# Router logits with the experts as columns of the result: four plain fp32 products in four column quarters of TensorE

## The chip, the cores and the metric

The kernel runs on one core of one Trainium2 chip. The metric is the device time of one launch in microseconds (us). TensorE is the matrix engine, VectorE, ScalarE and GpSimd work on its results, SyncE issues most of the transfers. In the profile they are PE (with PEld for its weight loads), DVE, ACT, POOL and SP.

## The reference

The input is 32 sequences of 512 tokens with 256 channels. Each sequence goes through two blocks, both as x = x + layernorm(block(layernorm(x))): first a state space block (a projection, a convolution along time, a scan in chunks, an output projection), then a mixture of experts with 16 routed experts and a shared one. The change is in the router:

```
logits = xf @ router_w.T                 # [tokens, 16]
scores = jax.nn.sigmoid(logits)
sb = scores + correction_bias            # 4 groups of 4 experts, best 2 groups, then best 4 experts
...
combine = jnp.zeros((S, E), xf.dtype).at[jnp.arange(S)[:, None], topk_idx].add(w)
g = jnp.einsum('sc,ech->esh', xf, gate_w)
u = jnp.einsum('sc,ech->esh', xf, up_w)
h = jax.nn.silu(g) * u
hw = h * combine.T[:, :, None]
```

## The kernel before, in words

**Stages.** The work of a sequence is cut into parts: p (norm, query projection, rotation), a (state space block, norm, sum), f (router and experts) and g (the end of the expert sum, last norm, store). One pass through `iteration` runs p of sequence i+1, a of sequence i, f of sequence i-1 and g of sequence i-2, all mixed. There are two filling passes and a first one with f, then a loop over 29 passes with all parts, and three emptying ones. A sequence has 12 blocks of 128 hidden units: `gate(j)` and `up(j)` make them, `down(j)` projects them back. `down(10)` and `down(11)` of a pass are done in the next one, as part g.

**Precision.** A matrix product is made of three one-pass products (type fp32r) of rounded high parts and low parts: high by high, high by low, low by high (`split_mm`). So each operand is rounded by ScalarE (its high part) and subtracted by VectorE (its low part). A few products are plain fp32: the states (`state`, `from_state`), `diagonal`, `CB` and the sums of `cumulate` (lines 1393 to 1395). Transpositions are products with an identity.

**The router.** `ffn_by_channel(0)` and `(1)` transpose the normed activations of each half of the tokens, ScalarE's `f_high` and VectorE's `f_low` make fTh and fTl of them. `logits(0)` and `logits(1)` use `narrow`: for each tile of 128 tokens and each half of the channels the tokens are the weights of the array, and the router's 32 columns (high and low parts of 16 experts) or 16 columns (high parts only) stream through. These are 16 products per sequence (lines 1374 and 1376). VectorE's `route_logits` adds the two column groups in two small instructions, ScalarE takes the tanh, VectorE picks the experts.

**What sets the order.** Every engine runs its own list, written out in `iteration` of that engine, and waits on counted semaphores. On TensorE these are waits for an operand (`read_out`, `wait_ge`) and for a PSUM bank to be free (`slot`): part p has one bank, a three, f two, in the order of P_SLOTS, A_SLOTS and F_SLOTS. The tuples FREED list in which order ScalarE and VectorE free the banks.

**The seam between two passes.** TensorE ends a pass with `gate(11)`, `h_by_channel(1)` and `up(11)`. The transposed h of the next sequence becomes hTh (ScalarE, `h_high`) and hTl (VectorE, `h_low`); `project_z(0, 0)` of the next pass waits until both halves of hTl are made. VectorE's `up(11)` multiplies the last hidden block out of PSUM.

```
if c == 0 and n == 0:
    pe.wait_ge(s_hT, 2)
    pe.sem_inc(s_hT, -2)
```

On VectorE the end of the list is `norm_q(1); h_low(0)`, `add_x(1)`, `h_low(1)`, `up(11)`; on ScalarE `gate(10)`, `h_high(0); h_high(1)`, `gate(11)`, `norm_x1(0)`, `round_hidden(10)`, `norm_x1(1)`, `round_hidden(11)`. TensorE begins a pass with `project_z(0, 0)`, `project_z(1, 0)`, `ffn_by_channel(0)`, which reads what `norm_x1(0)` made, `project_x(4)` and `ffn_by_channel(1)`.

Of the kernel before, what the change touches and what calls it, by code (L numbers as in the profile page):

```python
# [12 lines left out]
P = 128  # L13
# [19 lines left out]
def build(nc, x, wq_t, wzx_t, conv_w, conv_b, dt_bias, a_log, d_param, npw, ngw, wo_t,  # L33
# [6 lines left out]
    with ctx:  # L40
# [85 lines left out]
        junk = (xc[:, 4, :], xdec[:, 1, :])  # L126

# [10 lines left out]
        def rows(ap, dims, offset=0):  # L138
# [14 lines left out]
            ("za0", "DVE", "ACT"), ("za1", "DVE", "ACT"), ("xc4", "ACT", "ACT"), ("za2", "DVE", "ACT"),  # L153
            ("xc5", "ACT", "ACT"), ("za3", "DVE", "ACT"), ("xc0", "ACT", "ACT"), ("xc1", "ACT", "ACT"),
            ("xc2", "ACT", "ACT"), ("zb0", "ACT", "ACT"), ("acs", "DVE", "DVE"), ("zb1", "ACT", "ACT"),
            ("xc3", "ACT", "ACT"), ("Bt", "ACT", "ACT"), ("zb2", "ACT", "ACT"), ("CB", "ACT", "ACT"),
            ("xt0", "DVE", "DVE"), ("xt1", "DVE", "DVE"), ("st0", "DVE", "DVE"), ("zb3", "ACT", "ACT"),
            ("yd0", "DVE", "DVE"), ("yo1", "DVE", "DVE"), ("st1", "DVE", "DVE"), ("xt2", "DVE", "DVE"),
            ("yd1", "DVE", "DVE"), ("yo2", "DVE", "DVE"), ("yT0", "ACT", "DVE"), ("st2", "DVE", "DVE"),
            ("yd2", "DVE", "DVE"), ("xt3", "DVE", "DVE"), ("out0", "", "DVE"), ("yT1", "ACT", "DVE"),  # L160
            ("yo3", "DVE", "DVE"), ("yT2", "ACT", "DVE"), ("yd3", "DVE", "DVE"), ("out1", "", "DVE"),
            ("yT3", "ACT", "DVE")]
        F_SLOTS = [
            ("fT0", "ACT", "DVE"), ("fT1", "ACT", "DVE"), ("logits", "", "DVE"), ("G0", "ACT", "ACT"),
            ("U0", "DVE", "DVE"), ("G1", "ACT", "ACT"), ("U1", "DVE", "DVE"), ("G2", "ACT", "ACT"),
            ("U2", "DVE", "DVE"), ("G3", "ACT", "ACT"), ("G4", "ACT", "ACT"), ("U3", "DVE", "DVE"),
            ("cT", "ACT", "ACT"), ("U4", "DVE", "DVE"), ("G5", "ACT", "ACT"), ("U5", "DVE", "DVE"),
            ("G6", "ACT", "ACT"), ("U6", "DVE", "DVE"), ("G7", "ACT", "ACT"), ("U7", "DVE", "DVE"),
            ("G8", "ACT", "ACT"), ("U8", "DVE", "DVE"), ("G9", "ACT", "ACT"), ("U9", "DVE", "DVE"),
# [190 lines left out]
        def _(sp):  # L360
# [73 lines left out]
            def iteration(i, p, a, f, g):  # L434
                if f: save_x1(i - 1)
                if a: decay_store(); decay_rows(0); decay_rows(1)
                if f: combine_store(); combine_rows(0)
                if p: load_next(i + 1)
                if f: combine_rows(1)
                if a: decay_rows(2); decay_rows(3)  # L440
# [1224 lines left out]
```

## Time and profile before

| | us |
|---|---|
| median of 3 runs | 3214.55 |
| lowest and highest | 3213.54, 3217.93 |
| the profiled execution | 3218.34 |
| its span, first to last instruction | 3216.4 |
| TensorE busy | 3116.9 (97%) |
| VectorE busy | 2393.1 (74%) |
| GpSimd busy | 2033.7 (63%) |
| ScalarE busy | 1931.1 (60%) |

The busy time of an engine is the time in which it has at least one instruction under way. Matmuls overlap, so the time that one takes of the engine is the distance between its start and the start of the next one, not its duration.

### The profile page before, as it was taken

Reading aid. Unit: us, or ns where it says so; the run is one execution under the profiler, and the core shown is the slowest. Engines: PE = TensorE matmul, PEld = TensorE weight load, DVE = VectorE, ACT = ScalarE, POOL = GpSimd, SP = SyncE. Lnnn points to the kernel's source line nnn. Section 1 sums busy time; section 2 is a strip of 40 time slices with the busy share of each in tenths; the row PEclk is TensorE's granted clock in tenths of the full one; section 3 lists DMA queues with packets and bytes.
Section 4 is the critical chain, followed back from the end, with each engine's and each line's share of the span. In section 5 each row is a group of like instructions: output and inputs, shape, how many; then the busy total and the mean of one; then the engine's idle time right before and its main releaser. Section 6 shows DMA issues by size and latency. Waiting matters only on the chain.

```text
span 3216.4 us, 62379 instructions
## 1 busy us (share of the span) xinstructions
PE 3116.9 (97%) x19648; PEld 2723.4 (85%) x19648; DVE 2393.1 (74%) x5104; ACT 1931.1 (60%) x4146; POOL 2033.7 (63%) x2311
## 2 busy tenths in 40 slices
PE   3699999999999999999999999999999999999997
PEld 3588888888888888888888888888888888888886
DVE  3777777777777777777777777777777777777772
ACT  3566665566665566665666665666665656665652
POOL 0466666766666776666776666776666776666764
PEclk9799999999999999999999999999999999999999
DMA  3122222222222222222222222222222222222221
GB/s 109 40 70 80 66 59 74 73 76 79 66 60 75 72 77 78 66 60 74 72 78 76 66 63 72 72 79 76 66 65 71 71 79 76 66 67 69 71 80 40
DMA packets 143434, 227.33 MB, mean 71 GB/s; under 512 B 18977, under 2 KB 88353, under 8 KB 143393
## 3 DMA queue, kind: packets, MB, share of 16 engines
q1 hardware_dynamic: 126496, 210.06, 19.9%
q0 software_dynamic: 16896, 16.78, 4.0%
q8 instruction: 20, 0.33, 0.0%
q14 instruction: 22, 0.17, 0.0%
HBM read 174.87 MB, written 35.13 MB: 65 GB/s over the span
## 4 chain that ended last, share of the span: by engine, by line
PE 94%; POOL 1%; DMA 0%; DVE 0%; ACT 0%; issue 0%; SPq 0%; POOLq 0%; ACTq 0%; DVEq 0%
PE fpb L1325 33%; PE apb L1325 19%; PE acc L1504 17%; PE apb L1450 7%; PE apb L1334 4%; PE ppb L1325 3%; PE apb L1435 3%; PE apb L1442 2%; PE ppb L1344 2%; PE apb L1422 1%; PE fpb L1374 1%; PE fpb L1344 1%; PE fpb L1376 1%; PE fpb L1483 0%; PE apb L1395 0%; POOL hid L541 0%
## 5 line engine op out<-in xcount | busy, mean ns | idle before, releaser
L546 POOL TENSOR_TENSOR hidL<-hid,hidH 128x512 fp32r<-128x512 f32 x384 | 545.8, 1421 | 216.8 <-ACT hidH L801 207.5
L1015 DVE SCALAR_TENSOR_TENSOR xc<-apb,cw,xc 128x511 f32<-128x511 f32 (+2 forms) x576 | 427.8, 748 | 67.8 <-ACT xc L714 39.5
L1504 PE MATMUL acc<-WDH,hidH 128*128 128x256 f32 x1536 | 458.2, 298 | 6.2 <-POOLq L548 5.9
L801 ACT CAST hidH<-hid 128x512 fp32r<-128x512 f32 x384 | 236.1, 615 | 353.6 <-POOL hid L541 288.7
L1504 PE MATMUL acc<-WDH,hidL 128*128 128x256 f32 x1536 | 432.0, 281 | 0.0
L1504 PE MATMUL acc<-WDL,hidH 128*128 128x256 f32 x1536 | 431.5, 281 | 0.0
L541 POOL TENSOR_TENSOR hid<-hid,cb 128x512 f32<-128x512 f32 x256 | 347.2, 1356 | 81.8 <-DVEq L1136 43.7
L1134 DVE TENSOR_TENSOR hid<-hid,fpb 128x512 f32<-128x512 f32 x384 | 261.1, 680 | 135.4 <-PE fpb L1325 125.2
L1325 PE MATMUL fpb<-fTh,UH 128*128 128x512 f32 x768 | 336.1, 438 | 0.8 <-ACTq L793 0.8
L732 ACT ACTIVATE seg<-seg,acs 128x128 f32<-128x128 f32 x1024 | 313.8, 389 | 10.2 <-ACT cb L782 5.9
L1325 PE MATMUL fpb<-fTh,GH 128*128 128x512 f32 x768 | 317.5, 413 | 0.0
L1504 PEld LDWEIGHTS acc<-WDH,hidH 128*128 128x128 f32 x1536 | 290.6, 189 | 22.9 <-POOLq L548 8.6
L1325 PE MATMUL fpb<-fTh,GL 128*128 128x512 f32 x768 | 303.9, 396 | 0.0
L1325 PE MATMUL fpb<-fTh,UL 128*128 128x512 f32 x768 | 303.7, 395 | 0.0
L1325 PE MATMUL fpb<-fTl,UH 128*128 128x512 f32 x768 | 302.3, 394 | 0.0
L1325 PE MATMUL fpb<-fTl,GH 128*128 128x512 f32 x768 | 302.3, 394 | 0.0
L1504 PEld LDWEIGHTS acc<-WDL,hidH 128*128 128x128 f32 x1536 | 291.1, 189 | 12.8 <-issue 7.4
L790 ACT ACTIVATE hid<-fpb 128x512 f32<-128x512 f32 x384 | 228.5, 595 | 122.1 <-PE fpb L1325 84.1
L1504 PEld LDWEIGHTS acc<-WDH,hidL 128*128 128x128 f32 x1536 | 290.5, 189 | 0.0
L1450 PEld LDWEIGHTS apb<-xdt,seg 128*128 128x128 f32 x2048 | 245.9, 193 | 10.6 <-issue 5.1
L1450 PE MATMUL apb<-xdt,seg 128*128 128x64 f32 x2048 | 245.0, 273 | 3.6 <-DVE seg L1052 3.6
L1052 DVE TENSOR_TENSOR seg<-seg,CBs 128x1024 f32<-128x1024 f32 x128 | 195.5, 1528 | 41.9 <-ACT seg L732 32.5
(194 smaller groups left out, 8672.1 us busy)
## 6 DMA issues: line engine op xcount, KB each, us to landing
seg<-acs_row SPq DMA_DIRECT2D x128, 512.0 KB, 4.2
cb<-c_row SPq DMA_DIRECT2D x512, 128.0 KB, 2.9
xsP<-in_x SPq DMA_DIRECT2D x32, 512.0 KB, 3.6
xc<-qrot SPq DMA_DIRECT2D x32, 512.0 KB, 3.4
xc<-in_x SPq DMA_DIRECT2D x32, 512.0 KB, 4.3
out<-xc SPq DMA_DIRECT2D x32, 512.0 KB, 3.0
out<-xn POOLq DMA_DIRECT2D x32, 512.0 KB, 6.0
ZL_loaded<-in_wzx_t SPq DMA_DIRECT2D x2, 512.0 KB, 5.7
```

Of the source, the lines that this page charges most:

```text
L541: G.tensor_tensor(hid[:, j % 2, :], hid[:, j % 2, :], cb[:, r % 2, :], ALU.mult).then_inc(sem["routed_ready"], 1)
L546: own.do(G.tensor_tensor(hidL[:, j % 2, :], hid[:, j % 2, :], hidH[:, j % 2, :].bitcast(fp32), ALU.subtract))
L732: ins = A.activation(seg[:, c % 2, h, :], seg[:, c % 2, h, :], ACT.Exp, bias=acs[:, 0, c * HS + h:c * HS + h + 1])
L790: own.do(A.activation(hid[:, j % 2, :], bank(f"G{j}")[:], ACT.Silu))
L801: A.copy(hidH[:, j % 2, :], hid[:, j % 2, :]).then_inc(sem["hidden_high"], 1)
L1015: ins = V.scalar_tensor_tensor(xc[:, b, s:], src[:, 0:T - s], cw[:, b, TAPS - 1 - s:TAPS - s], xc[:, b, s:], ALU.mult, ALU.add)
L1052: V.tensor_tensor(seg[:, c % 2, :, :], seg[:, c % 2, :, :], CBs[:, c, :].unsqueeze(1).broadcast_to([P, HS, P]), ALU.mult).then_inc(sem["m_ ...
L1134: own.do(V.tensor_tensor(hid[:, j % 2, :], hid[:, j % 2, :], bank(f"U{j}")[:], ALU.mult))
L1325: ins = nc.tensor.matmul(dst, l, r, start=n == 0, stop=n == total - 1)
L1334: ins = nc.tensor.transpose(b[:, t * P:(t + 1) * P], src(t), ident[:])
L1450: ins = nc.tensor.matmul(b[:, hs], seg[:, c % 2, h, :], xdt[:, c % 2, hs], start=True, stop=True)
L1504: ins = nc.tensor.matmul(dst, l[:, w, tk], r[:, j, :], start=j == 0 and t % 2 == 0 and n == 0, stop=j == HB - 1 and n == 2, skip_group_che ...
```

## The change

The two calls of `logits` per sequence become one. The router's weights are now the stationary operand (32 columns: 16 high parts and 16 low parts), and all 512 tokens stream through. There are four such products, plain fp32: fTh and fTl, each with two halves of the channels. Product n writes rows 32n to 32n+31 of one PSUM bank, so each has its own quarter of the array's columns, and none is added to another in PSUM. ScalarE copies the bank [128, 512] to SBUF (`evac_logits`, into a free half of xdec), TensorE transposes it by four tiles of 128 tokens (`logits_by_token`, bank LT), and one VectorE sum over the eight parts of each expert (4 products by high and low) gives the logits. `narrow` goes.

With it the order lists of all engines are other ones, and so are the bank lists. The core of the diff, with the ends and beginnings of the lists:

```diff
-            def logits(s):
-                b = bank("logits") if s else slot("logits")
-                read_out(f"fT{s}")
-                ins = narrow(b, fTh, fTl, R, E, (2 * s, 2 * s + 1))
-                if s:
-                    ins.then_inc(sem["logits_made"], 1)
+            def logits():
+                b = slot("logits")
+                for s in range(2):
+                    read_out(f"fT{s}")
+                for n, (part, k) in enumerate(((fTh, 0), (fTh, 1), (fTl, 0), (fTl, 1))):
+                    ins = nc.tensor.matmul(b[n * 2 * E:(n + 1) * 2 * E, :], R[:, k, :].bitcast(fp32), part[:, k, :].bitcast(fp32),
+                                           start=True, stop=True)
+                fill("logits", ins)
+
+            def logits_by_token():
+                b = slot("LT")
+                read_out("logits")
+                fill("LT", transposes(b, lambda t: lgT[:, t * P:(t + 1) * P]))
...
+            def evac_logits():
+                filled(act, "ACT", "logits")
+                free("f", "logits", A.copy(lgT, bank("logits")[:]))
...
             def route_logits():
-                dve.wait_ge(sem["logits_made"], 1)
-                parts = bank("logits")[:, 0:2 * NT * E].rearrange("p (t a e) -> p t a e", t=NT, a=2)
-                own.do(V.tensor_copy(msk[:].rearrange(te, t=NT), parts[:, :, 0, :]))
-                own.do(V.tensor_tensor(msk[:].rearrange(te, t=NT), msk[:].rearrange(te, t=NT), parts[:, :, 1, :], ALU.add))
-                free("f", "logits")
+                filled(dve, "DVE", "LT")
+                parts = bank("LT")[:].rearrange("p (t n e) -> p t e n", t=NT, e=E)
+                own.do(V.reduce_sum(msk[:].rearrange(te, t=NT), parts, AX.X))
+                free("f", "LT")
                 dve.sem_inc(sem["logits_ready"], 1)
```

TensorE's list, its beginning:

```diff
+                if f: ffn_by_channel(0)
                 if w: weights_split(KD + 1)
-                if a: project_z(0, 0); project_z(1, 0)
-                if f: ffn_by_channel(0)
-                if a: project_x(4)
+                if a: project_z(0, 0)
                 if f: ffn_by_channel(1)
-                if g: down(10)
-                if f: settled("ffn_in_ready")
-                if a: project_z(2, 0); project_x(5)
-                if g: down(11); settled("last_split")
-                if f: logits(0); logits(1)
-                if a: project_z(3, 0); project_x(0)
-                if f: gate(0)
...
+                if a: project_z(1, 0)
+                if f: settled("ffn_in_ready")
+                if a: project_x(4); project_x(5)
+                if f: logits(); gate(0); logits_by_token()
+                if a: project_x(0)
+                if g: down(10)
+                if f: gate(1)
+                if a: project_z(0, 1); project_z(2, 0)
+                if f: up(0)
+                if a: project_z(1, 1); project_z(3, 0)
+                if g: down(11); settled("last_split")
```

Its end stays: `gate(11)`, `h_by_channel(1)`, `up(11)`. VectorE's end, and ScalarE's:

```diff
                 if p: norm_q(1); h_low(0)
                 if a: add_x(1)
                 if w: split_low(11)
+                if f: up(11)
                 if p: h_low(1)
-                if f: up(11)
...
                 if f: gate(10)
-                if p: h_high(0); h_high(1)
+                if p: h_high(0)
                 if f: gate(11)
+                if p: h_high(1)
                 if a: norm_x1(0)
```

In the middle ScalarE's list also changes: the four `exp_seg` of a pass stood in two groups between table loads (0 and 1, 2 and 3) and stand in three (0; 1 and 2; 3), so that a pass has eight table loads instead of six. On SyncE the load of `decay_rows(1)` stands ahead of `decay_rows(0)`, and the loads of the combine rows stand later among the others.

## Rows read from the trace of the kernel before

**Rows 1.** The page: busy time of TensorE, and the chain that ended last.
```profile
PE 3116.9 (97%) x19648; PEld 2723.4 (85%) x19648; DVE 2393.1 (74%) x5104; ACT 1931.1 (60%) x4146; POOL 2033.7 (63%) x2311
...
PE 94%; POOL 1%; DMA 0%; DVE 0%; ACT 0%; issue 0%; SPq 0%; POOLq 0%; ACTq 0%; DVEq 0%
```

**Rows 2.** Busy time in one pass: stretch, length, engines, granted clock, DMA share, GB/s.
```profile
1016.05:1112.45 96.40, 96.36 (x614) 84.50 (x615) 74.19 (x159) 59.80 (x130) 63.35 (x73) 1.00 0.24 71
```

**Rows 3.** TensorE's groups by line: the products of the logits.
```profile
L1376 PE MATMUL fpb<-R,fTl 128*128 128x16 f32 x256 | 58.2, 256 | 0.0
L1374 PE MATMUL fpb<-R,fTh 128*128 128x32 f32 x256 | 55.8, 252 | 0.4 <-DVE fTl L1118 0.4
```

**Rows 4.** TensorE in order of time around the logits: start, duration, engine, line, operation.
```profile
1024.88 0.18 PE L1374 MATMUL fpb<-R,fTh 128*128 128x32 f32 x1
...
1026.59 0.37 PE L1325 MATMUL apb<-ZH,hTh 128*128 128x264 f32 x1
1026.79 0.28 PE L1325 MATMUL apb<-ZL,hTh 128*128 128x264 f32 x1
1026.91 0.29 PE L1325 MATMUL apb<-ZH,hTl 128*128 128x264 f32 x1
```

**Rows 5.** TensorE in order of time: plain fp32 products of 512 columns.
```profile
1063.02 1.02 PE L1435 MATMUL apb<-S,xc 128*128 128x512 f32 x2
1063.87 1.02 PE L1442 MATMUL apb<-xdec,Btok 128*128 128x512 f32 x2
```

**Rows 6.** TensorE in order of time: around a product with 32 active columns.
```profile
1038.02 0.39 PE L1394 MATMUL apb<-ad,ones 128*128 128x32 f32 x2
1038.34 0.41 PE L1395 MATMUL apb<-upper,ad 128*32 128x128 f32 x2
1038.67 0.50 PE L1325 MATMUL fpb<-fTh,GH 128*128 128x512 f32 x1
1039.01 0.39 PE L1325 MATMUL fpb<-fTl,GH 128*128 128x512 f32 x1
```

**Rows 7.** TensorE in order of time: the seam of two passes.
```profile
1015.39 0.39 PE L1325 MATMUL fpb<-fTl,UH 128*128 128x512 f32 x1
1015.61 0.40 PE L1325 MATMUL fpb<-fTh,UL 128*128 128x512 f32 x1
1016.05 0.36 PE L1325 MATMUL apb<-ZH,hTh 128*128 128x264 f32 x1
...
1017.60 0.60 PE L1344 MATMUL fpb<-ident,xdt 128*128 128x128 f32 x4
1017.95 0.48 PE L1325 MATMUL apb<-hTh,ZH 128*128 128x512 f32 x1
1018.27 0.39 PE L1325 MATMUL apb<-hTl,ZH 128*128 128x512 f32 x1
```

**Rows 8.** VectorE in order of time: the seam; in brackets idle time and its releaser.
```profile
1011.02 0.69 DVE L1134 TENSOR_TENSOR hid<-hid,fpb 128x512 f32<-128x512 f32 x1 [0.81 <-PE fpb L1325]
1011.95 0.62 DVE L981 TENSOR_SCALAR xn<-qrot,rq 128x256 f32<-128x256 f32 x2 [0.24 <-DVE hid L1134]
...
1015.26 0.69 DVE L992 TENSOR_TENSOR hTl<-ppb,hTh 128x512 fp32r<-128x512 f32 x1
1016.12 0.69 DVE L1134 TENSOR_TENSOR hid<-hid,fpb 128x512 f32<-128x512 f32 x1 [0.17 <-PE fpb L1325]
```

**Rows 9.** ScalarE in order of time: the seam.
```profile
1014.64 0.59 ACT L703 CAST hTh<-ppb 128x512 fp32r<-128x512 f32 x1 [2.67 <-PE ppb L1344]
1015.13 0.60 ACT L790 ACTIVATE hid<-fpb 128x512 f32<-128x512 f32 x1
1015.92 1.09 ACT L768 ACTIVATE xdt<-xc,nb,rstd 128x256 f32<-128x256 f32 x2 [0.19 <-ACT hid L790]
```

**Rows 10.** ScalarE's groups by line: table loads, the rounding of yT, the copy of cT.
```profile
L655 ACT ACT_TABLE_LOAD x97 | 124.5, 1283 | 8.0 <-ACT hid L790 5.3 <-POOL one L466 1.4
...
L754 ACT CAST yTh<-apb 128x512 fp32r<-128x512 f32 x128 | 74.6, 583 | 90.8 <-PE apb L1334 88.9
...
L782 ACT COPY cb<-fpb 16x512 f32<-16x512 f32 x32 | 18.4, 575 | 47.5 <-PE fpb L1483 47.5
```

More of the change, by code:

```diff
@@ L152, in build @@
         A_SLOTS = [
[L153 to L157, printed above, removed]
@@ L166, in build @@
[L166 to L169, printed above, removed]
-            ("G10", "ACT", "ACT"), ("U10", "DVE", "DVE"), ("G11", "ACT", "ACT"), ("U11", "DVE", "DVE")]
+            ("fT0", "ACT", "DVE"), ("fT1", "ACT", "DVE"), ("logits", "ACT", "ACT"), ("G0", "ACT", "ACT"),
@@ L1546, in iteration @@
[L1546 to L1547 removed]
+                if a: settled("ad_ready"); project_x(3)
+                if f: up(2); gate(3); down(0); settled("acc_free"); gate(4)
+                if a: project_z(3, 1)
+                if f: down(1)
                 if a: CB(); x_by_token(0)
[L1549 removed]
+                if f: up(3); down(2)
+                if a: B_by_token()
+                if f: gate(5)
                 if a: x_by_token(1)
[L1551 removed]
@@ L1552, in iteration @@
-                if a: state(0); project_z(3, 1); diagonal(0)
-                if f: up(5)
-                if a: from_state(1); state(1)
-                if f: down(3)
-                if a: x_by_token(2)
-                if f: gate(6)
+                if f: combine_by_expert()
+                if a: state(0); diagonal(0)
+                if f: down(3); settled("c_ready")
+                if a: from_state(1)
+                if f: up(4)
+                if a: x_by_token(2); state(1); y_by_channel(0)
@@ L1558, in iteration @@
+                if f: up(5); gate(6)
+                if p: x_by_channel(0)
                 if a: diagonal(1); from_state(2)
-                if f: up(6); down(4)
-                if a: y_by_channel(0)
+                if f: down(4)
+                if a: state(2); x_by_token(3)
+                if f: up(6)
+                if a: settled("a_out_ACT", "xdec_ready")
                 if f: gate(7)
-                if a: state(2)
-                if f: up(7)
-                if a: settled("xdec_ready"); diagonal(2); x_by_token(3)
@@ L1573, in iteration @@
+                if a: project_out(1)
+                if f: gate(9)
                 if p: project_q(0)
-                if a: project_out(1)
-                if f: down(6); up(8)
-                if a: y_by_channel(2); diagonal(3)
+                if a: diagonal(3); y_by_channel(2)
+                if f: up(8)
+                if a: settled("m_ready")
                 if f: down(7)
-                if a: settled("m_ready")
                 if p: x_by_channel(1)
-                if f: gate(9)
+                if a: project_out(2)
```

250 lines of the change are left out of this document (122 added, 128 removed).

## The prediction

> **What bounds the kernel now.** I read the busy times first: TensorE has work under way for 97% of the span, and 94% of the chain that ended last runs through it [rows 1]. A share of busy time says little with overlapping matmuls, so I next took one pass of the loop by windows. It lasts 96.40 us, TensorE is busy for 96.36 of it at a granted clock of 1.00 (its upper level, 2.4 GHz), VectorE for 74.19, ScalarE 59.80, GpSimd 63.35 [rows 2]. The reader is to see that TensorE's list is the clock of the kernel: what it gains or loses in a pass comes 30 times, and what other engines gain or lose counts only where it makes TensorE wait. Then I looked in order of time for starts that are further apart than the same kind of product needs. There is one such place per pass worth naming, the seam: the last record of `up(11)` starts at 1015.61, products of 512 columns follow each other at 0.23, so the next could start at 1015.84; `project_z(0, 0)` starts at 1016.05 [rows 7], 0.10 after the end of the second hTl at 1015.95 [rows 8]. So 0.21 us per pass are lost there, to exactly the operand that the new lists touch.
>
> **Removed: sixteen narrow products.** They start at 1024.88 and the second product of the next projection starts at 1026.79; without them it would start one pitch of 0.12 after 1024.88, at 1025.00 [rows 4]. That is 1.79 us per sequence (0.112 each, far below their duration of 0.25 [rows 3]).
>
> **Added: four transpositions.** Four like them and the product behind them take 1017.60 to 1018.27, 0.67 us, of which 0.23 are that product's [rows 7]: 0.44 us.
>
> **Added: four plain fp32 products.** Such a product is two records of the trace. With 512 columns two records take 1063.02 to 1063.87, 0.85 us, so 0.43 each [rows 5]. How four in different quarters stand to each other no row shows. The ends: one behind the other, 8 x 0.43 = 3.44 us; all four at once, 2 x 0.43 = 0.86 us. I take a value between. The nearest row is the sum with 32 active columns: its two records use the same quarter and do not run together [rows 6], as they can't, since they need the same cells. If TensorE also starts its products strictly in the order of the list, as every row shows it to, the second record of product 0 waits for the first, the first of product 1 starts beside it and not before, and so on: a staircase of five steps, 5 x 0.43 = 2.15 us.
>
> The Trainium skill (TensorE: Matmul & The Clock Gate, Part 3: Packing small matmuls) says that matmuls in different column quarters run together at a few ns from each other, and that starts and ends keep program order; no row here has two quarters in use. Taken for the product as a whole that is the end of 0.86; taken for each record it is the staircase.
>
> **Added: into and out of 32 columns.** From 1038.02 to 1039.01, 0.99 us, lie two records at 0.112 (the pitch of the narrow ones), two of 128 columns at a quarter of 0.43, 0.107, and one of 0.23 [rows 6]: 0.67 by sum. The other 0.32 us is what the change of shape costs around them: the array empties before and after, and the next weights aren't loaded ahead. That comes once per sequence.
>
> **Sum of the router on TensorE.** 2.15 + 0.32 + 0.44 - 1.79 = +1.12 us per sequence, times 32 = +36 us. With the ends: 0.86 gives -0.17, or -5 us; 3.44 gives +2.41, or +77 us.
>
> **Moved: the seam.** This is the part that I am surest of. `up(11)` stays the last work of TensorE's pass, and VectorE now multiplies it before it makes the second half of hTl. The last record of U11 starts at 1015.61; VectorE takes it up at 1016.12 and ends at 1016.81 [rows 7, 8]. What follows such a multiplication starts 0.24 after its end (1011.71 to 1011.95 [rows 8]), so hTl is made from 1017.05 to 1017.74 by its 0.69, and `project_z(0, 0)` starts 0.10 later, at 1017.84 instead of 1016.05. Of the work that follows, only `ffn_by_channel(0)`, 0.44 us, is now ahead of it. Loss per seam: 1.79 - 0.44 = 1.35 us. Its cover would be other TensorE work, but the list has none that doesn't need hTl. `ffn_by_channel(0)` itself must start by 1017.40 to stay in that shadow. It needs `norm_x1(0)`, which ended at 1017.01 [rows 9]; now `gate(11)` goes first on ScalarE, from about 1014.3, then `h_high(1)`, so the norm ends near 1016.6. Not late. There are 30 seams whose earlier pass has both parts: +40 us. Ends: if ScalarE's gate is not early and the whole row of rounding, gate and norm is late, fT0 ends later by 0.3 and it is 1.65 (+50); if VectorE took the second operation with no gap, 1.1 (+33).
>
> **Other engines.** ScalarE gets a copy of 128x512 (0.58 for a like one) and two more table loads at 1.28 [rows 10]: 3.1 us per pass, 63 of 96 us busy. It must be done within `gate(0)`'s 1.4 us after the products: about 0.2 to see the bank and 0.6 for itself; and where the queue still holds `conv_first(5)` (0.78) it ends before the staircase does. VectorE's two instructions of 0.22 become one over 512 elements, 0.2 to 0.5 more, with 22 us free per pass. `down(11)` ends some 10 us later in a pass, and with it the last moments, the last norm and the release of the accumulators; `down(0)` waits for that, stands later too, and I count its release a good microsecond ahead. SyncE's `decay_rows(0)` lands one transfer later, ahead of an `exp_seg(0)` that stands behind a table load. I walked the list from the seam to `diagonal(0)` with the durations of the rows, and find each operand ready by 0.2 us or more; the tightest is `diagonal(0)` itself. I take 0 for all this; the ends are -0.15 us per pass (the idle of 0.36 that sums of pitches leave in 96.40, without the seam's 0.21) and +0.6 (one operation of ScalarE or VectorE late, once), -5 to +18 us. Filling and emptying the pipeline may move some us either way.
>
> **The sum.** 3218.34 + 36 + 40 = 3294 on the profiled execution, which is 3.8 above the median; on the median 3291 us, +2.4%.
>
> **The rivals.**
> A. The four quarters run one behind the other: +77 instead of +36, 3332 us. For it: no row shows two products at once, and every plain fp32 record takes its full 0.43. Against: different cells, different PSUM rows.
> B. All four run at once, products as wholes: -5 instead of +36, 3250 us. For it: there is no shared cell; against: it needs the first record of product 1 to start before the second of product 0.
> C. Faster: the seam is covered. This is one mechanism: hTl lands within 0.65 us of the last start of U11 (0.23 plus `ffn_by_channel(0)`), since what `h_low(1)` waits for was done long before; then the 0.21 of today goes as well, 30 x 0.21 = 6, and with all quarters at once 5 more: 3203 us. It decides at 1016.28 on the clock of rows 7. For it: the transposition was moved into that gap. Against: VectorE works in order, and U11 is seen by it only at 1016.12.
> D. No change: B, and the seam is no wider than today's 0.21, 3214.55 - 5 = 3210 to 3220 us. It needs C's mechanism by half.
> E. A second wait of more than 0.6 us in each pass on top: 3340 and above.
>
> **How the numbers follow.** Forecast (staircase and seam) 0.40, own range 3275 to 3312; A 0.22; B 0.23; C 0.06; D 0.04; E 0.05. The range 3242 to 3340 holds the forecast, A and B and leaves out C, D and E, 0.15. What a measurement of this kernel can tell from no change is about 0.2%, 6.4 us. Faster 0.07, same 0.05, slower 0.88.
>
> **What will show it.** Right: in the profile after, TensorE's first `project_z` of a pass starts 0.1 behind the second hTl of VectorE, that hTl stands behind the multiplication of U11, and the page shows a wait of TensorE of more than a microsecond per pass at that place (for hTl, or for `ffn_by_channel(0)`'s input). A pass is 98.9 us. The eight records of the logits start in five steps of 0.43, with two starts close together at the inner ones; eight steps are A, two groups of four are B. The transpositions take 0.44 and the first product behind the router comes 0.1 late with its load. Wrong: a pass under 97 us; hTl of `h_low(1)` ahead of U11's product; new waits at `diagonal`, `down(0)` or `logits_by_token` that are larger than the seam.

## The result, and the profile after

The changed kernel took 3300.0 us (median of 4 runs, 3299.9 to 3301.5); the kernel before took 3216.2 us (4 runs, 3213.5 to 3220.3). The ratio is 1.026, with a 95% interval of 1.0243 to 1.0278. It is slower, and 9 us from the forecast of 3291. The profiled execution has a span of 3298.1 us at a mean granted clock of 0.99, where the one before had 3216.4: 81.7 us more.

The busy times on the page after. TensorE's share has fallen from 97% to 95%, though it is busy for 26 us more; the rest of the loss is idle time.

```profile
span 3298.1 us, 62218 instructions
...
PE 3142.8 (95%) x19520; PEld 2679.0 (81%) x19520; DVE 2466.6 (75%) x5072; ACT 2059.7 (62%) x4242; POOL 2045.4 (62%) x2311
```

One pass of the loop, in the columns of [rows 2]:

```profile
1038.07:1136.80 98.73, 97.13 (x610) 83.08 (x610) 76.70 (x159) 63.87 (x133) 63.88 (x73) 1.00 0.24 70
```

A pass is 98.73 us instead of 96.40, at the same granted clock of 1.00, so 2.33 us longer; 30 of them are 70 us. From the last logits to the end of the program it takes 88.4 us where it took 76.3: 12 us. These two are the whole difference. Of the 2.33 us of a pass, 1.56 are idle TensorE: it is busy for 97.13 of 98.73.

TensorE in order of time at the seam, to be read against [rows 7]:

```profile
1134.67 0.40 PE L1335 MATMUL fpb<-fTh,UL 128*128 128x512 f32 x1
1135.98 0.66 PE L1354 MATMUL fpb<-ident,xdt 128*128 128x128 f32 x4 [0.91 <-DVEq L936]
1136.90 0.36 PE L1335 MATMUL apb<-ZH,hTh 128*128 128x264 f32 x1 [0.26 <-issue]
```

`project_z(0, 0)` starts 2.23 us after the last record of U11, where before it started 0.44 after. The forecast was 1015.61 to 1017.84, also 2.23. The bracket shows something the forecast didn't have: `ffn_by_channel(0)` (the four transpositions) waits too, 0.91 us idle, until VectorE has given a PSUM bank back.

VectorE and then ScalarE in the same stretch, against [rows 8] and [rows 9]:

```profile
1135.18 0.69 DVE L1139 TENSOR_TENSOR hid<-hid,fpb 128x512 f32<-128x512 f32 x1 [0.99 <-PE fpb L1335]
1136.11 0.69 DVE L998 TENSOR_TENSOR hTl<-ppb,hTh 128x512 fp32r<-128x512 f32 x1 [0.24 <-DVE hid L1139]
...
1138.77 0.17 DVE L1003 TENSOR_TENSOR dr<-apb,dtb 128x8 f32<-128x8 f32 x1 [1.97 <-DVEq L317]
```

```profile
1137.47 0.62 ACT L802 CAST hidH<-hid 128x512 fp32r<-128x512 f32 x1 [0.28 <-POOL hid L542]
1139.16 0.59 ACT L771 CAST fTh<-fpb 128x512 fp32r<-128x512 f32 x1 [1.08 <-ACTq L317]
1139.65 0.39 ACT L739 ACTIVATE zs<-apb 128x256 f32<-128x256 f32 x1
```

VectorE does what the new list says: U11's product first, from 1135.18, then, 0.24 after its end, hTl until 1136.80; the projection starts 0.10 later. ScalarE's last operation of the pass is the rounding of U11's hidden values at 1137.47, for it comes behind the product on VectorE and the weighting on GpSimd. Then ScalarE stands for 1.08 us while the semaphores of the pass are settled, and only at 1139.16 does it begin the first work of the next pass, the rounding of fT0.

The router on TensorE, against [rows 4]:

```profile
1141.44 0.40 PE L1335 MATMUL apb<-hTh,ZL 128*128 128x512 f32 x1
1141.77 0.62 PE L1479 MATMUL fpb<-fTh,R 128*32 128x512 f32 x2
1141.78 0.62 PE L1479 MATMUL fpb<-fTl,R 128*32 128x512 f32 x2
1142.22 0.60 PE L1479 MATMUL fpb<-fTh,R 128*32 128x512 f32 x2
1142.24 0.60 PE L1479 MATMUL fpb<-fTl,R 128*32 128x512 f32 x2
1142.77 0.50 PE L1335 MATMUL fpb<-fTh,GH 128*128 128x512 f32 x1
1143.11 0.39 PE L1335 MATMUL fpb<-fTl,GH 128*128 128x512 f32 x1
```

Each row with "x2" joins two records. Taken singly they start at 1141.769, .776, .783, .789 and then at 1142.223, .229, .236, .243: two groups of four, 7 ns apart inside a group. The first record of every product runs, all four at once, and then the second of every product. From the last start before them (1141.44) to the second product behind them (1143.11) it takes 1.67 us; with no router it would be two pitches of 0.23, so the products and the change of shape cost 1.20 us. With 0.44 for the transpositions and without the 1.79 of the narrow products that is -0.15 us per sequence. There was no staircase.

What TensorE waits for in the other places (engine, line, releaser; total us, times, longest):

```profile
PE fpb L1354 <- DVEq L936: 28.3, 31, 0.9
PE ppb L1335 <- DVE xTl L967: 13.0, 33, 2.3
```

In order of time, `from_state(2)` and the first product of `project_q(1)`:

```profile
1092.70 1.10 PE L1435 MATMUL apb<-S,xc 128*128 128x512 f32 x2
...
1122.67 0.36 PE L1335 MATMUL ppb<-WQH,xTh 128*128 128x256 f32 x1 [0.26 <-DVE xTl L967]
```

The table of waits puts 0.26 of idle time at `project_q(1)`, but idle time begins where the modelled end of a matmul lies. Measured by starts, as at the seam, the product starts 0.50 us later than it does where nothing holds it (0.03 behind the last transposition, in e7_xlow_first below). `from_state(2)`, at 1092.70, shows no bracket at all and comes 0.43 us behind the last record of `diagonal(1)` where it comes 0.11 behind it in the kernel before; with 0.02 more at its second record it is 0.34 late. Both stand behind VectorE. VectorE in order of time, and GpSimd in the same stretches:

```profile
1072.22 3.33 DVE L1188 TENSOR_TENSOR gt<-gt,eq 128x64 f32<-128x64 f32 x1
...
1088.16 2.12 DVE L1058 TENSOR_TENSOR seg<-seg,CBs 128x1024 f32<-128x1024 f32 x1
1090.20 1.58 DVE L1069 TENSOR_TENSOR S<-S,el 128x512 f32<-128x512 f32 x1
1091.81 0.69 DVE L1072 TENSOR_TENSOR S<-S,apb 128x512 f32<-128x512 f32 x1
...
1118.40 2.48 DVE L1110 SCALAR_TENSOR_TENSOR xc<-xc,rstd 128x256 f32<-128x256 f32 x2 [0.31 <-DVE hid L1139]
```

```profile
1072.80 2.66 POOL L502 TENSOR_SCALAR_AFFINE_SELECT seg<-seg 128x1024 f32<-128x1024 f32 x2
...
1087.90 1.30 POOL L542 TENSOR_TENSOR hid<-hid,cb 128x512 f32<-128x512 f32 x1
1089.15 2.08 POOL L502 TENSOR_SCALAR_AFFINE_SELECT seg<-seg 128x1024 f32<-128x1024 f32 x1
...
1117.89 1.28 POOL L518 TENSOR_TENSOR zs<-zs,xD 128x512 f32<-128x512 f32 x1
1119.13 1.47 POOL L542 TENSOR_TENSOR hid<-hid,cb 128x512 f32<-128x512 f32 x1
```

Three of these groups of VectorE take far longer than their kind does elsewhere in the same trace (the product of seg and CBs 1.22, that of S and el 0.69, the two of xc and rstd 0.87), and each lies beside instructions of GpSimd. The operands of `from_state(2)` and `project_q(1)` come out of these lists. But the stretch is not new. The kernel before has it in the same places, `new_state(1)` and `add_x(0)`:

```profile
1065.06 1.45 DVE L1052 TENSOR_TENSOR seg<-seg,CBs 128x1024 f32<-128x1024 f32 x1
1066.43 1.77 DVE L1063 TENSOR_TENSOR S<-S,el 128x512 f32<-128x512 f32 x1
...
1096.22 0.69 DVE L961 TENSOR_TENSOR xTl<-ppb,xTh 128x512 fp32r<-128x512 f32 x1 [0.79 <-ACT xTh L691]
1096.83 2.27 DVE L1104 SCALAR_TENSOR_TENSOR xc<-xc,rstd 128x256 f32<-128x256 f32 x2
```

What is new is what stands in front. Before, xTl was made ahead of the slow `add_x(0)`, now it is made behind it. And `times_dt(2)`, two instructions of 0.69 us, stood behind `new_state(1)` and now stands ahead of `decay_CB(1)`, whose product of seg and CBs takes 2.12 where it took 1.45.

### The profile page after: what moved, and what is told of

It reads as the page before. It is cut to its first block and busy times, and to the rows that moved or that the text cites. A ratio compares the mean times of both kernels' runs of the same rounds, so it can differ in the third digit from the quotient of the medians.

```text
span 3298.1 us, 62218 instructions
## 1 busy us (share of the span) xinstructions
PE 3142.8 (95%) x19520; PEld 2679.0 (81%) x19520; DVE 2466.6 (75%) x5072; ACT 2059.7 (62%) x4242; POOL 2045.4 (62%) x2311
## 5 line engine op out<-in xcount | busy, mean ns | idle before, releaser
L547 POOL TENSOR_TENSOR hidL<-hid,hidH 128x512 fp32r<-128x512 f32 x384 | 526.0, 1370 | 306.9 <-ACT hidH L802 280.0
L1513 PE MATMUL acc<-WDH,hidH 128*128 128x256 f32 x1536 | 453.9, 296 | 11.3 <-POOLq L549 10.8
L802 ACT CAST hidH<-hid 128x512 fp32r<-128x512 f32 x384 | 237.5, 618 | 240.0 <-POOL hid L542 163.3
L1139 DVE TENSOR_TENSOR hid<-hid,fpb 128x512 f32<-128x512 f32 x384 | 262.3, 683 | 163.7 <-PE fpb L1335 153.8
L542 POOL TENSOR_TENSOR hid<-hid,cb 128x512 f32<-128x512 f32 x256 | 336.8, 1316 | 46.3 <-DVEq L1141 32.5
```

The costliest lines, as they stand in the source:

```text
L542: G.tensor_tensor(hid[:, j % 2, :], hid[:, j % 2, :], cb[:, r % 2, :], ALU.mult).then_inc(sem["routed_ready"], 1)
L547: own.do(G.tensor_tensor(hidL[:, j % 2, :], hid[:, j % 2, :], hidH[:, j % 2, :].bitcast(fp32), ALU.subtract))
L802: A.copy(hidH[:, j % 2, :], hid[:, j % 2, :]).then_inc(sem["hidden_high"], 1)
L1139: own.do(V.tensor_tensor(hid[:, j % 2, :], hid[:, j % 2, :], bank(f"U{j}")[:], ALU.mult))
L1513: ins = nc.tensor.matmul(dst, l[:, w, tk], r[:, j, :], start=j == 0 and t % 2 == 0 and n == 0, stop=j == HB - 1 and n == 2, skip_group_che ...
```

## The experiments

Each kernel was timed on one chip with the kernel before: e1 to e4 together, e5 to e8 together, e9 to e11 together. The kernel before took 3219.1, 3219.2 and 3220.0 us there. "Pass" is the mean distance of the logits' first records over the 29 full passes, "tail" the time from the last logits to the end. In this measure the kernel before has 96.40 and 76.3 us, the changed one 98.73 and 88.4. "By starts" means that the distance of two starts on TensorE is compared with the distance of the same two where nothing holds them.

### e1_seam_vector: the swap undone on VectorE

```
-                if f: up(11)
                 if p: h_low(1)
+                if f: up(11)
```

> The changed kernel with one swap on VectorE: h_low(1) again ahead of up(11). Everything else as changed. Theory 1 (two waits lie on top of each other at the seam: project_z(0, 0) waits for hTl, and ffn_by_channel(0) ahead of it waits until VectorE has read U11, because the added bank LT moved U11 and fT0 to the same PSUM bank): the second stays, fT0 starts 1.3 us after the last start of U11 as now, and only the 0.47 us between fT0 and project_z goes, 30 x 0.47 = 14 us: 3286 us against 3300. Rival (only hTl holds the seam, as the prediction had it): 30 x 1.35 = 40 us less, 3260 us.

Measured: 3302.6 us, ratio 1.0261 (1.0246 to 1.0277), pass 98.78. Neither theory came: nothing came back. `ffn_by_channel(0)` starts 1.45 us after the last U11 (1430.35 to 1431.80), 0.14 later than in the changed kernel, since VectorE now frees U11's bank second. `project_z(0, 0)` follows it closely, 0.36 us earlier after U11 than in the changed kernel. But `project_x(5)`, further down TensorE's list, gives 0.41 back. It starts 5.57 us after the last U11 (at 1435.92); in the changed kernel it starts 5.61 after it (1134.67 to 1140.28), without a wait of its own. Something else holds it at the same place, and the next experiment shows what.

### e2_seam_both: the swap undone on VectorE and TensorE

```
-                if f: ffn_by_channel(0)
...
-                if a: project_z(0, 0)
-                if f: ffn_by_channel(1)
-                if a: project_z(1, 0)
+                if a: project_z(0, 0); project_z(1, 0)
+                if f: ffn_by_channel(0); ffn_by_channel(1)
```

> The swap on VectorE of the last kernel and on TensorE project_z(0, 0) and project_z(1, 0) ahead of ffn_by_channel(0) and (1), which is the seam of the kernel before. Theory 1 (hTl and the bank of U11 are all that the seam costs): a pass is 1.35 us shorter than 98.72, 97.37, and the kernel takes 3300 - 40 = 3260 us. Rival (the projections ahead delay fT0, its rounding and so the logits): part comes back as a wait at the logits, 3275 us or more.

Measured: 3301.4 us, ratio 1.0261 (1.0247 to 1.0275), pass 98.79. Again nothing came back, as the rival's "3275 us or more" had it, though the seam itself closed and the wait is not at the logits. TensorE in order of time:

```profile
1431.02 0.40 PE L1335 MATMUL fpb<-fTh,UL 128*128 128x512 f32 x1
1431.87 0.36 PE L1335 MATMUL apb<-ZH,hTh 128*128 128x264 f32 x1 [0.45 <-issue]
...
1436.59 0.49 PE L1335 MATMUL apb<-hTh,ZH 128*128 128x512 f32 x1 [0.75 <-ACT zs L739]
```

`project_z(0, 0)` now starts 0.85 after the last U11 instead of 2.23, and 4.7 us later `project_x(5)` waits 0.9 for the bank that ScalarE's `silu_z(0, 0)` frees (it starts at 1436.15, after the rounding of U11's values at 1433.97 and that of fT0 at 1435.66). That instruction hangs on the chain U11, VectorE's product (L1139), GpSimd's weighting (L542), ScalarE's rounding (L802), and the 1.08 us of settling. From the last U11 to ScalarE's first work of the next pass this chain takes 4.64 us here and in e1_seam_vector, 4.49 in the changed kernel and 4.50 in the kernel before. `project_x(5)` starts 5.57 us after U11 again. So the seam has two holders, hTl and this chain, and they end within 0.04 us of each other (5.61 and 5.57): taking the first away leaves the wait to the second.

### e3_router_alone: only the new router, in the kernel before

```
-                if f: logits(0); logits(1)
+                if f: logits()
...
-                if f: gate(0)
+                if f: logits_by_token(); gate(0)
```

It also has the copy on ScalarE, the sum on VectorE and the additional bank; all lists keep the order of the kernel before, but that `route_logits` stands behind the last moments.

> The kernel before with the new router alone: its own order lists, with the four products at the place of the old ones, the copy behind silu_z(2, 0), the transpositions after project_x(0), the sum after the last moments. Theory 1 (the router itself is cheaper on TensorE, 1.10 + 0.44 instead of 1.79 us, and all of the loss is order): a pass of 96.15 us instead of 96.40, the kernel 8 us faster than before, 3207 us. Rival (the longer way of the logits over ScalarE and TensorE costs waits wherever it stands): a pass of 96.4 or more, no gain.

Measured: 3214.2 us (11 runs), ratio 0.9985 (0.9976 to 0.9994), pass 96.26, tail 77.3. The records of the router stand as in the changed kernel, in two groups of four that start at 1312.99 and 1313.44.

The router by itself is a gain of 0.14 us per pass (0.25 was expected), 5 us in all, as rival B of the prediction had it. The whole loss of the changed kernel therefore comes from the new order of the lists.

### e4_other_waits: the waits of `project_q(1)` and `from_state(2)`, on e2_seam_both

```
-                if a: times_dt(2); decay_CB(1)
+                if a: decay_CB(1)
...
-                if a: new_state(1)
+                if a: new_state(1); times_dt(2)
...
+                if p: x_low(1)
                 if a: add_x(0)
...
-                if p: x_low(1)
```

The list in which VectorE frees the banks is changed to match.

> The last-but-one kernel (the changed one with the seam of before) and two more edits on VectorE: x_low(1) ahead of add_x(0), and times_dt(2) behind new_state(1) instead of ahead of decay_CB(1). Theory 1 (what is left of the loss per pass is two waits of TensorE, 0.50 us at project_q(1) for xTl and 0.39 us at from_state(2) for the state, both behind VectorE instructions that ran 0.9 to 1.6 us longer while GpSimd was busy): a pass of 96.5 us, 27 us less than with the seam alone, 3233 us. Rival (the waits move to the next product, since VectorE's list is as full as before): less than 10 us.

Measured: 3296.6 us, ratio 1.0244 (1.0230 to 1.0258), pass 98.53. The rival came. Both waits went, 0.50 and 0.35, and a new one came, for `times_dt(2)` now frees its bank late:

```profile
PE apb L1450 <- DVE xD L1053: 11.0, 31, 1.7
```

By starts it is 0.57 us at `diagonal(1)`. So 0.85 less 0.57 should have given 0.28; the pass gave 0.26. In this kernel the product of S and el at `new_state(1)` takes 0.68 us and that of seg and CBs 1.23, so the place of `times_dt(2)` and the stretch went together, and this run doesn't tell them apart.

### e5_seam_three_lists: ScalarE's list as well, on e2_seam_both

```
-                if f: f_high(0)
                 if a: silu_z(0, 0)
-                if f: f_high(1)
+                if f: f_high(0); f_high(1)
...
-                if p: h_high(0)
+                if p: h_high(0); h_high(1)
...
-                if p: h_high(1)
```

> The changed kernel with the seam of before on VectorE (h_low(1) first) and TensorE (both projections first), as in the second experiment, and now on ScalarE too: h_high(1) ahead of gate(11), and at the start of a pass silu_z(0, 0) ahead of f_high(0). Theory 2 (the second experiment won nothing since project_x(5), now fourth in TensorE's pass, needs the bank that silu_z(0, 0) frees, and that stands behind the chain U11, VectorE's up(11), GpSimd's combine(11), ScalarE's round_hidden(11), 1.1 us of semaphore work at the end of ScalarE's pass and f_high(0); only the f_high, 0.5 us, is taken out of it here): a pass of 98.3 us, 3287 us. Rival (hTl at project_z and the order of f_high were the two missing pieces): a pass of 97.4, 3260 us.

Measured: 3291.3 us, ratio 1.0224 (1.0208 to 1.0240), pass 98.47. `project_z(0, 0)` has its 0.45 after the last U11 again and the wait of `project_x(5)` is gone, but two others hold the head of the pass, the second `ffn_by_channel` and the logits, 0.64 and 0.31 us by starts:

```profile
1429.14 0.63 PE L1352 MATMUL fpb<-ident,xdt 128*128 128x128 f32 x4 [0.44 <-ACT xdt L765]
...
1432.92 0.62 PE L1477 MATMUL fpb<-fTh,R 128*32 128x512 f32 x2 [0.23 <-DVE fTl L1122]
```

That is close to the 98.3 of theory 2. Three lists have the seam of before and still a pass is only a third of a microsecond shorter: what is missing is work of TensorE to lie beside the chain (the next kernel shows it).

### e6_down_ahead: `down(10)` back to the head of the pass, on e5_seam_three_lists

```
-                if f: ffn_by_channel(0); ffn_by_channel(1)
+                if f: ffn_by_channel(0)
+                if a: project_x(4)
+                if f: ffn_by_channel(1)
+                if g: down(10)
...
-                if a: project_x(4); project_x(5)
+                if a: project_x(5)
...
-                if g: down(10)
```

> The last kernel, and TensorE has down(10) between ffn_by_channel(1) and project_x(5), with project_x(4) ahead of ffn_by_channel(1), as the kernel before has it: 1.4 us of work while ScalarE gets to silu_z(0, 0). Theory 2: project_x(5) doesn't wait any more, a pass is 1.35 us shorter than the changed one, 97.4 us, 3260 us. Rival (some other chain through the emptying of the lists holds 98.7 us, and TensorE's waits only move): 3285 us or more.

Measured: 3257.3 us, ratio 1.0122 (1.0107 to 1.0138), pass 97.37, tail 86.2. The 12 records of `down(10)` are 1.4 us of work that needs nothing from this chain, and with them ahead of `project_x(5)` the waits of the head are gone. From e2_seam_both to here a pass loses 1.42 us: this is the size of the seam that the forecast had (1.35), got back by four edits together. Each of the first three was worth nothing or 0.32; whether `down(10)` at the head would do with fewer of them beside it was not tested.

### e7_xlow_first: `x_low(1)` ahead of `add_x(0)`, on e6_down_ahead

```
+                if p: x_low(1)
                 if a: add_x(0)
...
-                if p: x_low(1)
```

> The last kernel with x_low(1) ahead of add_x(0) on VectorE. Theory: the wait of 0.50 us at project_q(1) is the whole cost of add_x(0) standing ahead, which GpSimd stretches from 0.9 to 2.5 us; it goes: 15 us less than the last kernel, 3245 us. Rival (add_x(0) later moves the wait to its own readers, or the pass is held by another chain): less than 5 us.

Measured: 3241.1 us, ratio 1.0071 (1.0057 to 1.0085), pass 96.86, tail 84.2. The pass loses 0.51, what `project_q(1)` waited; its first product comes 0.50 us earlier behind the transpositions, and no other distance of two starts changes by more than 0.02. VectorE in order of time in this kernel:

```profile
1391.50 0.69 DVE L965 TENSOR_TENSOR xTl<-ppb,xTh 128x512 fp32r<-128x512 f32 x1 [1.72 <-ACT xTh L688]
1392.11 0.88 DVE L1108 SCALAR_TENSOR_TENSOR xc<-xc,rstd 128x256 f32<-128x256 f32 x2
```

Both gains are there: xTl comes first, and the two instructions of `add_x(0)`, 2.48 us in the changed kernel, now take 0.88: the instructions of GpSimd beside them work on two elements per partition, not on 512. One edit changed both the place and the stretch. In the place of the changed kernel, the 2.27 us of the kernel before would still have made `project_q(1)` some 0.3 late (an estimate: 0.50 less 0.21), and 0.88 not at all. The wait took both: the old stretch and the new place.

### e8_mask_later: GpSimd's `mask(2)` behind `rest(4)`, on e7_xlow_first

```
-                if a: mask(2)
                 if f: rest(4)
-                if a: decayed(2)
+                if a: mask(2); decayed(2)
```

> The last kernel with GpSimd's mask(2) behind rest(4) instead of ahead of it. Theory (VectorE's instructions with two operands in SBUF stand still while GpSimd works in SBUF; mask(2) met decay_CB(1), 2.1 instead of 1.2 us, and the scaling of the state, 1.6 instead of 0.7, and that is the wait of 0.39 us at from_state(2)): decay_CB(1) takes 1.2 us again, from_state(2) waits less than 0.1, 9 to 12 us less than the last kernel. Rival (rest(4) comes into the same place and stretches the same instructions): no change.

Measured: 3249.3 us, ratio 1.0098 (1.0083 to 1.0114), pass 97.18. It is 8 us slower than e7_xlow_first, where the theory had a gain and the rival no change. VectorE in the stretch of `new_state(1)`:

```profile
1362.08 2.10 DVE L1055 TENSOR_TENSOR seg<-seg,CBs 128x1024 f32<-128x1024 f32 x1
1364.11 1.75 DVE L1066 TENSOR_TENSOR S<-S,el 128x512 f32<-128x512 f32 x1
```

Another instruction of GpSimd takes the place of the mask (the one of `rest(4)`, from 1363.90 for 1.42 us), and the product of S and el takes 1.75 us instead of 1.57 (0.69 alone). The product of seg and CBs keeps its 2.1 us, so it was not the mask that stretched it. GpSimd works for two thirds of the pass; to push one instruction away brings the next. The wait of `from_state(2)` grew from 0.34 to 0.52, which is 0.18 of the 0.33 that the pass lost. Two more were stretched further on in the pass, a product of seg and CBs from 1.38 to 2.25 and the second one of S and el from 0.69 to 1.49, and a `gate` behind them starts 0.10 late.

### e9_one_quarter: all four products in one quarter, on e3_router_alone

```
+                    m = n % 1
-                    ins = nc.tensor.matmul(b[n * 2 * E:(n + 1) * 2 * E, :], R[:, k, :].bitcast(fp32), part[:, k, :].bitcast(fp32),
-                                           start=True, stop=True)
+                    ins = nc.tensor.matmul(b[m * 2 * E:(m + 1) * 2 * E, :], R[:, k, :].bitcast(fp32), part[:, k, :].bitcast(fp32),
+                                           start=n < 1, stop=n >= 3, skip_group_check=True)
```

The four products are summed in PSUM, and VectorE's sum has two terms in place of eight.

> The kernel before with the new router alone (third experiment, a pass of 96.25 us), but all four plain fp32 products go to rows 0 to 31, one quarter of the array's columns, and are added in PSUM; the sum on VectorE takes two parts instead of eight. Theory (products in one quarter follow each other, and the gain of the four quarters is that they run at once): eight records at 0.43, 3.44 us instead of 0.87; a pass of 98.8 us, the kernel 82 us slower than the third experiment, 3296 us. Rival (the time is that of streaming 512 tokens with 32 columns, whatever the quarters): no difference.

Measured: 3296.1 us, ratio 1.0239 (1.0224 to 1.0255), pass 98.78, as the theory had it. Eight records follow one another, at 0.453 us once and then at 0.429:

```profile
1343.60 1.90 PE L1476 MATMUL fpb<-fTh,R 128*32 128x512 f32 x4
1345.34 1.88 PE L1476 MATMUL fpb<-fTl,R 128*32 128x512 f32 x4
```

### e10_two_quarters: two products in each of two quarters, on e3_router_alone

```
+                    m = n % 2
-                    ins = nc.tensor.matmul(b[n * 2 * E:(n + 1) * 2 * E, :], ...
+                    ins = nc.tensor.matmul(b[m * 2 * E:(m + 1) * 2 * E, :], ...
-                                           start=True, stop=True)
+                                           start=n < 2, stop=n >= 2, skip_group_check=True)
```

Two products are added in PSUM in each quarter, and VectorE's sum has four terms.

> The same with two quarters: products 0 and 2 in the first, 1 and 3 in the second, added in PSUM. The order of the list alternates quarters. Theory A (records of different quarters run at once, and a record waits only for those of its own quarter): 4 steps of 0.43, 1.72 us; a pass of 97.1 us, 28 us slower than the third experiment. Theory B (TensorE keeps the order of the list record by record, which with four quarters it did not): a longer staircase, 5 steps or more, 2.15 us and more, 42 us or more slower.

Measured: 3240.8 us, ratio 1.0068 (1.0053 to 1.0084), pass 97.10, theory A. The records come in four steps of 0.43, two at each step, 7 ns apart:

```profile
1322.86 1.05 PE L1476 MATMUL fpb<-fTh,R 128*32 128x512 f32 x4
1323.74 1.03 PE L1476 MATMUL fpb<-fTl,R 128*32 128x512 f32 x4
```

With one, two and four quarters in use a pass is 98.78, 97.10 and 96.26 us. Between them the eight records take eight, four and two steps: 4 x 0.43 = 1.72 and 2 x 0.43 = 0.86 less, and 1.68 and 0.84 are measured. Quarters of the array divide the time, record by record.

### e11_one_pass: the same with the rounded type, in one quarter, on e9_one_quarter

```
-                    ins = nc.tensor.matmul(b[m * 2 * E:(m + 1) * 2 * E, :], R[:, k, :].bitcast(fp32), part[:, k, :].bitcast(fp32),
+                    ins = nc.tensor.matmul(b[m * 2 * E:(m + 1) * 2 * E, :], R[:, k, :], part[:, k, :],
```

The parts are kept in the rounded type already, so here they are multiplied without being read as plain fp32.

> The same as e9 with one quarter, but the products are of the one-pass type fp32r, as everywhere else in the kernel (all operands are rounded parts already, so nothing is lost but low by low rounding). Four records of 512 columns at 0.233 each: 0.93 us instead of the 0.87 of the four quarters. Theory: the same pass as the third experiment within 0.1 us, 96.25 to 96.35, so 0 to 3 us slower. Rival (with 32 columns a one-pass product costs as much as a plain record, or its weights are loaded in the open each time, 0.03 to 0.1 us): 96.4 to 96.6.

Measured: 3206.4 us, ratio 0.9961 (0.9947 to 0.9975), pass 96.00. It is the fastest kernel of all, 8 us ahead of e3_router_alone, where the theory had it up to 3 us behind: the theory kept the cost of the change of shape, and there is none here.

```profile
1308.09 0.29 PE L1510 MATMUL acc<-WDH,hidL 128*128 128x256 f32 x1
1308.21 0.63 PE L1476 MATMUL fpb<-fTh,R 128*32 128x512 f32 x2
1308.68 0.63 PE L1476 MATMUL fpb<-fTl,R 128*32 128x512 f32 x2
1309.15 0.29 PE L1331 MATMUL apb<-ZH,hTh 128*128 128x264 f32 x1
1309.27 0.29 PE L1331 MATMUL apb<-ZL,hTh 128*128 128x264 f32 x1
```

Each product is one record of 0.233 us, four take 0.93, and nothing is lost ahead of or behind them: 0.12 from the record before, 0.12 to the second one after. The four plain fp32 products are faster by themselves, 0.87 for all, but pay some 0.32 for the change of shape around them.

## Why the prediction was right, and where it wasn't

The time came within 9 us, in the predicted direction and range. That is in part luck. The sum behind it did not hold in the same way: the seam was right to a few hundredths of a microsecond; the router came out 41 us lower than forecast, and the two terms that were put at nothing or left open came to 46 us. The two errors cancel: with the router as measured and the other two at nothing, the time would have been rival B's 3250 us.

| term | forecast, us | measured, us | by |
|---|---|---|---|
| router, 32 sequences | +36 | -5 | e3_router_alone, e9 to e11 |
| seam, 30 passes | +40 | +40 (1.35 each by starts; 1.42 given back) | trace after; e6_down_ahead |
| other waits, 30 passes | 0 (-5 to +18) | +34 (1.13 each) | 0.50 and 0.34 by starts, 0.29 by subtraction; 0.51 given back by e7_xlow_first |
| emptying the pipeline | "some us either way" | +12 | trace after |
| sum | +76 | +81 (span: +81.7) | |

The 0.29 is what is left of the 2.33 us of a pass when the rest is taken off, so the sum of the last column agrees with the span by construction; it is no check of the terms.

**The bound.** Right. TensorE's list was the clock, and each of the eleven kernels has a span that differs from the one before by its pass times 30 and its tail, to within 4 us.

**The router.** Every term but one was right: 0.44 for the transpositions, 0.32 for the shape (e3_router_alone: 1.19 in all less 0.87), 1.79 for what was removed. The step that failed is "if TensorE also starts its products strictly in the order of the list ... a staircase of five steps". The start of product 1 doesn't wait for the second record of product 0: all first records run together and then all second ones, 0.87 in place of 2.15. This was rival B. The argument against it ("it needs the first record of product 1 to start before the second of product 0") was no row but a reading of how records must stand; the trace shows exactly that exchange.

The Trainium skill (TensorE: Matmul & The Clock Gate, Part 3: Packing small matmuls) says that matmuls in different column quarters run together a few ns apart. The trace agrees, with 7 ns. Its other statement, that starts keep program order, holds for products here, but not for their records.

**The seam.** Right in place and size, and the cause that was named is there: VectorE takes U11 first, hTl stands 0.24 behind, `project_z(0, 0)` starts 2.23 us after the last U11, as forecast. Two things were missed. With one bank more in the list of the FFN, U11 and the first transposition fall on the same bank, so `ffn_by_channel(0)` isn't the free cover it was taken for; it starts 1.08 us late by starts (0.91 of it idle), but still inside the shadow of the same wait, and the sum didn't change. And the seam was treated as one wait with one cause. The experiments show two holders, VectorE's order and the chain through GpSimd and ScalarE into the next pass: the first alone gives nothing back (e1, e2), four edits together 1.42 (e6). In the changed kernel the two end within 0.04 us of each other at `project_x(5)`. The named cause explains the 1.35, but the chain that was not seen would have cost as much by itself, with `down(10)` gone from the head of the pass. That the size came out right says little for the claim that hTl alone sets it.

**Other engines at nothing.** This step failed. The walk through the list found every operand ready with 0.2 us or more to spare; three came late instead. The prediction shows no duration of `add_x(0)`, `decay_CB(1)` or `new_state(1)`, so which ones the walk took can't be told. The trace of the kernel before had them: 2.27 us for the two instructions of `add_x(0)`, where the other two of the same line take 0.87, and 1.77 for the product of S and el. In the new order `add_x(0)` stands ahead of xTl and takes 2.48 us, and xTl comes late for `project_q(1)`: 0.50 per pass, shown by e7_xlow_first. Ahead of `from_state(2)` the products of seg and CBs and of S and el take 2.12 and 1.58 us, 0.48 more together than before, and the 1.3 us of `times_dt(2)` are new there: 0.34 per pass. Which of the two is its cause stays open: e4_other_waits moves `times_dt(2)` and removes wait and stretch together, but makes another wait; e8_mask_later lengthens both the product and the wait. The remaining 0.29 (some 0.1 of it at `diagonal(0)`) was not tested.

**The tail.** The forecast left it open. It became 12 us. In the emptying passes `down` waits for GpSimd's `rest`, 3.09 us in one place and 1.67 in another:

```profile
3240.90 0.58 PE L1513 MATMUL acc<-WDH,hidH 128*128 128x256 f32 x1 [3.09 <-POOLq L549]
```

All such waits of a run come to 10.8 us, where they come to 5.9 in the kernel before, so they account for 5 of the 12. That the tail belongs to the order and not to the router is shown by e3_router_alone, whose tail is 77.3 us. Which of the moved operations carries it stays open; in the kernels up to e7_xlow_first 4 us of it are gone.

**The views named as proof.** Of the signs of a right forecast, those of the seam came, with a pass of 98.73 us for the forecast 98.87. The sign for B (two groups of four) came instead of the five steps. The page did show waits of more than a microsecond per pass for the seam's place, but split over two holders, 0.91 and 0.26.

## What to carry to other kernels

Price the new instructions and the new order of the lists apart, and try each by itself: here the instructions gained 5 us, and the order lost some 87. Where a pass ends in a chain that goes through several engines, a wait at the seam has more than one holder: look for what TensorE can do beside it (here 1.4 us of `down`), before swapping single instructions. Where GpSimd is busy for two thirds of the time, don't walk a list with one duration per kind of instruction: here the same pair took 0.87 and 2.27 us in one pass of the kernel before, and 2.48 became 0.88 by a swap. Read each one's duration at its own place, and give what is moved both values. And try the one-pass type before four quarters: with operands that are rounded parts already it was 8 us faster here, and simpler.

## What the runs showed of the hardware

The longest stretch was that of one of the smallest instructions. Groups by line, before and after (count, then busy us and mean ns):

```profile
L1183 DVE TENSOR_TENSOR gt<-gt,eq 128x64 f32<-128x64 f32 x32 | 7.2, 225 | 1.1
```

```profile
L1188 DVE TENSOR_TENSOR gt<-gt,eq 128x64 f32<-128x64 f32 x32 | 97.2, 3039 | 1.1
```

The same instruction over 64 elements takes 225 ns before and 3039 after. In the kernel before two of its neighbours were the stretched ones instead (the scan into th with 1180 ns and the product of th and eq with 1022, which take 308 and 324 after). In the pass shown above it runs from 1072.22 to 1075.55, while GpSimd's two selects run from 1072.80 to 1075.46: it ends when they end. It starts 0.58 us ahead of them, though, beside GpSimd's issue of a transfer:

```profile
1071.92 1.38 POOL L568 DMA_DIRECT2D out<-xn  x1 [0.92 <-POOL hidL L547]
```

By itself it would have ended before the first select began. Whether the issue holds it as well, or whether GpSimd's times in the profile are too rough to tell, stays open. It reads two operands in SBUF, as do the others that were stretched. Products with one operand in PSUM kept their 0.69 us beside GpSimd in the same passes (1091.81 above; GpSimd makes hidL from 1091.21 to 1092.92).

The Trainium skill (SBUF — State Buffer, Who interferes with whom) says that VectorE and GpSimd share a port to SBUF under a lock, and that VectorE contends where both its inputs are in SBUF. The traces agree, with these numbers; they show the delay, not the lock.

At the end of each pass's list a settling of semaphores stands between two passes. On ScalarE the gap there is 1.08 us in the kernel before, in the changed one and in e2_seam_both. On VectorE it is 2.96, 1.97 and 2.85 us in these three, so it is no fixed price there; in all three its first work starts 0.6 to 0.75 us behind the end of ScalarE's last, so it may be a wait. The gap lies on the path only where the last operation of a pass and the first of the next belong to one chain, as here.

Changing to 32 active columns and back costs some 0.32 us with plain fp32 (e3_router_alone), and nothing that can be seen with the rounded type (e11_one_pass: 0.12 us ahead; the second product behind starts 1.06 after the first record, and four records and one pitch are 1.05). In the plain fp32 case the next weights are not loaded ahead: the load for the first `gate` product starts at 1142.76, with its product at 1142.77, and 0.84 us after the load before it ended.
